# One semaphore for all of TensorE's steps in a graph network kernel, raised at the end of a step, with the collecting matmuls moved there

## What is computed

```
ew = edge_attr @ edge_w + edge_b
for l in range(3):
    msg = relu(x[src] * ew)
    out = 0
    for i in range(3):
        h = segment_sum(msg * (edge_type == i), dst) * inv_cnt[i]
        out = out + h @ weights[l, i]
    out = out + x @ roots[l] + biases[l]
    x = x + relu(out)
return layernorm(x_in + x)
```

## Time and profile before

| | |
|---|---|
| median of 3 runs | 3626.61 us (3626.02 to 3627.41) |
| span of the profiled execution | 3632.0 us |
| instructions in it | 59677 |
| mean granted clock of TensorE | 0.895 |
| busy share of the span | PE 78%, PEld 72%, POOL 62%, DVE 59%, ACT 35% |
| gathers on GpSimd | 2346, 953 and 960 ns each on average |
| collect matmuls in the trace | 9384, 305 ns each |
| edge weight matmuls in the trace | 4692, 338 ns each |

### The profile page before, as it was taken

One profiled execution on the slowest core, in us unless ns is written; L12 is line 12 of the kernel. 1 busy time (PEld: TensorE's weight loads), 2 busy tenths in 40 slices (PEclk: granted clock), 3 DMA queues, 4 the chain that ended last, 5 costly groups with the idle time before them and its releaser, 6 DMA issues.

```text
span 3632.0 us, 59677 instructions
## 1 busy us (share of the span) xinstructions
PE 2818.6 (78%) x18430; PEld 2609.9 (72%) x18430; DVE 2148.2 (59%) x5997; ACT 1285.0 (35%) x2700; POOL 2256.5 (62%) x2368
## 2 busy tenths in 40 slices
PE   6777778888888777778777877777777777787777
PEld 5777777777777677777777777767666777777776
DVE  6666666666666555555555555545555665556566
ACT  6555555555555322222222222222222222222222
POOL 6666666666666466666666666646666666666664
PEclk9999999999999878888898888887888888888888
DMA  4444444444444344444444444434444444444443
GB/s 126 128 129 128 127 132 127 131 127 131 130 128 130 114 125 118 122 119 121 122 124 118 124 122 119 122 106 127 125 126 121 130 123 127 129 124 130 125 128 100
DMA packets 318631, 450.88 MB, mean 124 GB/s; under 512 B 155996, under 2 KB 205802, under 8 KB 318314
## 3 DMA queue, kind: packets, MB, share of 16 engines
q0 software_dynamic: 112608, 307.65, 29.8%
q1 hardware_dynamic: 205706, 139.36, 13.7%
HBM read 401.96 MB, written 44.82 MB: 123 GB/s over the span
## 4 chain that ended last, share of the span: by engine, by line
PE 61%; issue 16%; another core or an unknown queue 9%; DVE 8%; ACT 3%; DVEq 2%; POOL 1%; DMA 0%; POOLq 0%; SPq 0%
PE bank L800 31%; PE bank L781 14%; PE bank L849 13%; DVE acc L971 4%; PE bank L754 2%; DVE t L988 1%; DVE xg L1088 1%; ACT at L656 1%; PE bank L824 1%; ACT oh_a L702 1%; PE bank L795 1%; DVEq L1078 1%; DVEq L971 1%; DVE S L952 0%
## 5 line engine op out<-in xcount | busy, mean ns | idle before, releaser
L608 POOL DMA_INDIRECT xg<-x,idx x1564 | 1490.9, 953 | 897.3 <-issue 361.5
L800 PE MATMUL bank<-S,xg 128*128 128x96 f32 x9384 | 1459.0, 305 | 400.7 <-issue 197.4
L800 PEld LDWEIGHTS bank<-S,xg 128*128 128x128 f32 x9384 | 1324.2, 217 | 461.2 <-issue 441.2
L685 ACT ACTIVATE xg<-xg 128x512 f32<-128x512 f32 x1173 | 739.1, 630 | 2064.0 <-DVE xg L1088 1270.0
L971 DVE TENSOR_TENSOR acc<-acc,bank 128x192 f32 x2346 | 817.1, 348 | 767.0 <-PE bank L800 490.6
L1088 DVE TENSOR_TENSOR xg<-xg,bank 128x512 f32<-128x512 f32 x1173 | 802.0, 684 | 600.2 <-remote 273.5
L781 PE MATMUL bank<-wsb,at 128*128 128x256 f32 x4692 | 990.4, 338 | 213.8 <-issue 128.8
L608 POOL DMA_INDIRECT xg<-in_x_dram,idx x782 | 750.5, 960 | 451.0 <-PE bank L800 212.2
L781 PEld LDWEIGHTS bank<-wsb,at 128*128 128x128 f32 x4692 | 753.8, 214 | 286.7 <-issue 183.5
L849 PE MATMUL bank<-W,acc 128*128 128x256 f32 x1764 | 506.5, 411 | 2.2 <-issue 2.0
L849 PEld LDWEIGHTS bank<-W,acc 128*128 128x128 f32 x1764 | 385.5, 257 | 5.6 <-issue 2.0
(11 more groups left out here) (87 smaller groups left out, 728.2 us busy)
## 6 DMA issues: line engine op xcount, KB each, us to landing
at<-attr_t SPq DMA_DIRECT2D x390, 128.0 KB
xg<-x,idx POOLq DMA_INDIRECT x1564
attr_t<-at SPq DMA_DIRECT2D x195, 128.0 KB
xg<-in_x_dram,idx POOLq DMA_INDIRECT x782
hs<-in_edge_attr_dram SPq DMA_DIRECT2D x195, 64.0 KB
x<-t SPq DMA_DIRECT2D x96, 128.0 KB
xblk<-x SPq DMA_DIRECT2D x96, 128.0 KB
xblk<-in_x_dram SPq DMA_DIRECT2D x48, 128.0 KB
```

The lines of the kernel that those rows point to most:

```text
L608: eng.indirect_dma_start(out=xg[:, n % XR, :], out_offset=None, in_=xs[l], in_offset=bass.IndirectOffsetOnAxis(ap=idx[:, tile(j):tile(j) + ...
L685: eng.activation(v, v, ACT.Relu).then_inc(s_r, 1)
L800: last = eng.matmul(pA[V % 2][:, 192 * i + 96 * h:192 * i + 96 * h + 96], xg[:, n % XR, 128 * h:128 * h + 128], S[:, slot(l, 2 * q + i), : ...
```

## The change

All of those seven semaphores but one use of `s_tr` (the very first turn, before the loop) go. One semaphore, `s_step`, takes their place. TensorE raises it once in each step in which it has work, on the step's last matmul. Whoever waited for a kind of work now waits for the end of the step that holds it; a table `count_at` gives the number of that step. `weighed(Q)` is the step in which the edge weights of Q are made, which is the one before Q; `collected(V)` is the step after V; `attr_turned`, `mixed` and `stepped` do the same for the other kinds. In TensorE's loop the collect moves from behind the count to the end of the step, behind the products and the turns, so that it is a step's last work wherever there is one. No arithmetic changes, no buffer changes, and the other engines' streams keep their order.

```
+        def tensor_works(l, q):
+            return (0 <= q + 1 < NP or 0 <= q - 1 < NP or (l == 0 and (bool(starting(q, 1)) or q % 2 and 1 <= (q + 3) // 2 < NG))
+                    or any(q == turn_step(k) for k in range(NB))
+                    or any(q == mix_step(l, k, m) for k in range(NB) for m in range(R + 1)))
+        worked = [(l, q) for l in range(L) for q in range(-3, end) if tensor_works(l, q)]
+        count_at = {at: i + 1 for i, at in enumerate(worked)}
+        def stepped(l, q):
+            return count_at[l, q]
+        def weighed(Q):
+            return stepped(Q // NP, Q % NP - 1)
+        def collected(V):
+            return stepped(V // NP, V % NP + 1)
+        def attr_turned(g):
+            return stepped(0, 2 * g - 3)
+        def mixed(l, k, m):
+            return stepped(l, mix_step(l, k, m))
...
 # sync: reload_attr
-                eng.wait_ge(s_e, l * NP + 2 * max(0, g - TR + 1))
+                eng.wait_ge(s_step, weighed(l * NP + 2 * max(0, g - TR + 1) - 1))
...
 # gpsimd: gather
-                    eng.wait_ge(s_sc, 2 * ((n - XR) // 2 + 1))
+                    eng.wait_ge(s_step, collected((n - XR) // 2))
...
 # scalar: attr_copy, copy of a turned block, masks, clearing of acc
-                eng.wait_ge(s_tr, g + 1)
+                if g:
+                    eng.wait_ge(s_step, attr_turned(g))
...
-                            eng.wait_ge(s_xt, K + 1)
+                            eng.wait_ge(s_step, stepped(l, turn_step(k)))
...
-                                    eng.wait_ge(s_sc, j - AR + 1)
+                                    eng.wait_ge(s_step, collected((j - AR) // 2))
...
-                                eng.wait_ge(s_d1, NB * l + k + 1)
+                                eng.wait_ge(s_step, mixed(l, k, R))
...
 # tensor: every helper returns its last matmul in place of raising
-                last.then_inc(s_e, 1)
+                return last
...
-                    last.then_inc(s_sc, 1)
+                return last
...
                         if 0 <= q + 1 < NP:
-                            edge_weights(l, q + 1)
+                            last = edge_weights(l, q + 1)
                         if l == 0:
                             for k in starting(q, 1):
-                                count(k)
-                        if 0 <= q - 1 < NP:
-                            collect(l, q - 1)
+                                last = count(k)
                         for k in range(NB):
                             for m in range(R + 1):
                                 if q == mix_step(l, k, m):
-                                    mix(l, k, m)
+                                    last = mix(l, k, m)
                         if l == 0 and q % 2 and 1 <= (q + 3) // 2 < NG:
-                            attr_turn((q + 3) // 2)
+                            last = attr_turn((q + 3) // 2)
                         for k in range(NB):
                             if q == turn_step(k):
-                                turn_x(l, k)
+                                last = turn_x(l, k)
+                        if 0 <= q - 1 < NP:
+                            last = collect(l, q - 1)
+                        if tensor_works(l, q):
+                            last.then_inc(s_step, 1)
...
 # vector: adds, first op of a block, counts, multiplication
-                eng.wait_ge(s_sc, 2 * V + 2)
+                eng.wait_ge(s_step, collected(V))
...
-                    eng.wait_ge(s_d0, K + 1)
+                    eng.wait_ge(s_step, mixed(l, k, 1))
...
-                eng.wait_ge(s_cm, sum(p - 1 <= q for p in starts))
+                if q >= starts[0] - 1:
+                    eng.wait_ge(s_step, stepped(0, starts[sum(p - 1 <= q for p in starts) - 1] + 1))
...
-                            eng.wait_ge(s_e, Q + 1)
+                            eng.wait_ge(s_step, weighed(Q))
```

More of the change, by code:

```diff
@@ L186, in gnn_program @@
         s_g = sems("s_g", XR)
-        s_e, s_m, s_r, s_S, s_sc, s_acc = (sem(n) for n in ("s_e", "s_m", "s_r", "s_S", "s_sc", "s_acc"))
+        s_step, s_m, s_r, s_S, s_acc = (sem(n) for n in ("s_step", "s_m", "s_r", "s_S", "s_acc"))
         s_an = sems("s_an", 3)
@@ L191, in gnn_program @@
         s_at = sems("s_at", TR)
[L192 to L193 removed]
+        s_oh, s_ob, s_cn, s_inv, s_df = (sem(n) for n in ("s_oh", "s_ob", "s_cn", "s_inv", "s_df"))
         s_w = sem("s_w")
@@ L811, in count @@
                 eng.wait_ge(s_cn, min(NP, starts[k] - 1))
-                eng.matmul(pH[:, 4 * (k % 2):4 * (k % 2) + 3], diff[:, :], cnt[:, 3 * blocks[k]:3 * blocks[k] + 3],
-                           start=True, stop=True).then_inc(s_cm, 1)
+                return eng.matmul(pH[:, 4 * (k % 2):4 * (k % 2) + 3], diff[:, :],
+                                  cnt[:, 3 * blocks[k]:3 * blocks[k] + 3], start=True, stop=True)
             def turn_x(l, k):
@@ L825, in turn_x @@
                                          ident[0:n, 0:n])
-                last.then_inc(s_xt, 1)
+                return last
             def mix(l, k, m):
@@ L849, in mix @@
                     last = eng.matmul(o, a, W[:, 2 * (r % 4) + h, :], start=(h == 0), stop=(h == 1))
-                if m % 2:
-                    last.then_inc(pair_done[m // 2], 1)
-            pair_done = [s_d0, s_d1]
+                return last
             def fast():
@@ L1061, in count_ops @@
                 if i == 0:
-                    eng.wait_ge(s_cm, k + 1)
+                    eng.wait_ge(s_step, stepped(0, starts[k] + 1))
                     eng.tensor_scalar(v, pH[:, 4 * (k % 2):4 * (k % 2) + 3], 1.0, None, ALU.max).then_inc(s_inv, 1)
```

24 lines of the change are left out of this document (12 added, 12 removed).

## The result

The changed kernel takes 3736.18 us (3732.38 to 3737.89 in 4 runs) against 3626.83 us for the kernel before: a ratio of 1.0301, 95% interval 1.0286 to 1.0316. It is slower by 109 us, where 3570 us and a gain had been forecast. The time lies inside the range, at its upper end, but the forecast had the wrong sign, and the rival that gave almost this time (C, 3741 us) got there by a split that the trace refutes.

A forecast was written before the change was run, and what follows sets the result against it. The prediction took a convoy to bound the kernel: TensorE's raises, held while GpSimd issues gathers, come in bundles. 3632.0 less 55 for layers 1 and 2, zero elsewhere, gave 3577, less 5.4 is 3572, rounded to 3570 us; range 3480 to 3740.

The forecast's parts named there:

- Rival C: Slower: TensorE can't get as far ahead, giving gather stretches of two; +64 us layers 1 and 2, +50 layer 0; 3741 us, chance 0.30.
- The rhythm: GpSimd's gathers come in stretches, four in layer 0 (6.13 us), mostly six in layers 1 and 2 (8.99 us).
- Raises removed: TensorE raises fall from 4,204 to 1,189, so held raises pass sooner; layers 1 and 2 gain 780 x 0.07 = 55 us.
- the forecast's own sum, 0.41 + 4 x 2.86: GpSimd's gather stretches: each restart costs 0.41 us, each step 2.86 us; longer stretches pay the restart less often.
- The floor of 2.86 us a step: Lowest time a step that the gather rhythm allows, against 3.00 us in layers 1 and 2 and 3.06 in layer 0.
- Later signal for the weights: Multiplication waits for the whole previous step, not just its edge weights; two steps cover the lag, nothing in layers 1 and 2.
- Collect behind the products and turns: In TensorE's step the collect comes later, delaying GpSimd's release and SyncE's reloads; total work unchanged, costed at nothing.
- Layer 0, the turn of a block: 49 steps where the turn of x waits for ScalarE's attribute copy lengthen to 3.6 to 5.9 us; taken as zero.
- the landed gathers of some four steps: Layer 0: gathers already landed let a long turn step be made up, the reason for taking zero there.
- The counts: VectorE's addition of counts waits for the step's end 49 times; 18 us at most, in the range only.

## Why the prediction was wrong

**The rhythm was read rightly, its cause was not.** Bundled raises and stretches of four and six gathers are in both traces. The step that failed first is "Raises removed": it took the number of raises for what holds them back. With 28% of them layers 1 and 2 gained nothing, where 55 us were forecast; with half the gathers the lags went. The stretches of eight that were to show the forecast right did come, 47 where there were 4, but at 2.97 us a step against 3.00 they are worth next to nothing: the forecast's own sum, 0.41 + 4 x 2.86 = 11.85 us for such a stretch (11.9 measured), would have asked for stretches of twelve to gain 0.07 us a step. The prediction had named this test itself, "I am wrong at the root if the lags are the same with a quarter of the raises", and that is what came. The floor of 2.86 us a step held only where the lags are: 2.55 to 2.59 us under the quick condition, and 1.90 to 1.94 with half the gathers.

The Trainium skill, "TensorE: Matmul & The Clock Gate", section "The cost: per-tile semaphore tail", would have given 79 us for the raises, an estimate from its price. The traces of before and after show none of it in layers 1 and 2 (0.1 us). Under the quick condition a small price isn't ruled out: 1,167 raises given back cost 7 to 8 us, where the page's price would make an estimate of 30 us.

**"Later signal for the weights" was costed at nothing for layers 1 and 2, and the sum held**: a wait of the adds became a wait of the multiplication of the same pace. The argument for it did not. It let two steps, 5.7 us, cover a lag of 2.55 us at most, and lags of 4.6 us are in the same lines. The sum was right in part by luck, and a gain from fewer raises cancelled by the later signals isn't quite excluded; against it stand the 1169.6 and 1172.1 us with the weights' signal early again.

**"Collect behind the products and turns" was costed at nothing and was not.** The sum "nothing is added to a step but the order" overlooked that the turn of x waits inside its step, and that a collect put behind it waits with it. Alone that is 24 us.

**"Layer 0, the turn of a block" is the term that carried the result**, and it was put at zero, between ends of +140 and -40 us. The chain multiplication, relu, copy, turn, collect was put at 3.6 to 5.9 us with the lag, and 5.46 were counted. But the reason given, that the multiplication is now released by a step's end, is not what makes this step long: with the weights signalled early and only the collect moved it takes 5.45 us. It is the collect's place behind the turn, the term above. What the late weights' signal makes long was missed. The step behind is long too, 4.53 us (3.40 with the weights' own raise), because the split and the copy of the turned block both stand behind a multiplication that waits for the long step's end. And "the landed gathers of some four steps" could make up nothing: rows that have landed don't help a multiplication that waits for a raise. That buffer works only as long as the weights are signalled by themselves, as the kernel with the collect last shows. Measured, the term is +100.6 us. The counts are in it, and no run takes them apart.

**Rival C** gave 3741 us from +64 us in layers 1 and 2 and +50 in layer 0; the trace has 0 and +100. It was right that stretches of two would come (by count 98 in layer 0, where there were 4), and wrong where. The Trainium skill, "Perfetto Trace Analysis", section "Optimization Strategy", advises to make the dependency behind a gap start sooner or complete faster. The weights' raise, which signals one sooner, took the loss from 3.1 to 0.7%, and layer 0 from 1295.4 to 1206.3 us: there the runs agree. The turned block's raise also signals sooner and gave nothing.

How much of layer 0 is the clock's stays open. Its granted clock fell from 0.96 to 0.89 and TensorE's busy time rose by 67 us there; both follow the standing, and no run held the one and changed the other.

## What to carry to other kernels

Before merging semaphores, list for each waiter how much earlier its signal comes than the merged one, and look for instructions that wait inside the step: put nothing that others wait for behind them. A signal is worth only what the head of the waiting queue can use. To learn what sets a rhythm, halve one engine's work at a time: here half the gathers took a quarter off the time, and half of each product 0.2%.

## What the runs showed that I had not expected

TensorE's raises are seen late while GpSimd issues indirect gathers densely, under one of two conditions of the chip: for instance 2.55 us behind the matmuls in the trace before, and 2.20 in the one after, with a single raise a step. With half the gathers the adds wait only 20.8 us in a stretch of 1100. Under the other condition such lags are rare (in layer 1 of the kernel with one collect raise 9 adds waited, where 151 did in the trace before), and the kernel before takes 3096 instead of 3627 us. What makes the chip be in the one or the other isn't known; one and the same chip was found in both. It matters for verdicts: the changed kernel with the collect in its old place is 0.8% faster under the one and 1.1% slower under the other, and no kernel, other than those that leave work out, was seen faster than the kernel before under both. Two ran under the quick one alone.
